# Transformer layer on one core: later constants, the second x tile and query projection ahead of kv, a seven-step Newton, one score matmul per group, and the last down product and norm in column halves

## The chip, the cores and the metric

The kernel runs on one core of a Trainium2 chip. Its time is device microseconds of one execution. The kernel before takes 1866.86 us (median of 3 runs, 1866.0 to 1867.02). The profile is of another single execution, which took 1868.12 us; its span, from the first to the last instruction, is 1866.4 us. The engines are PE (TensorE), DVE (VectorE), ACT (ScalarE), POOL (GpSimd) and SP (SyncE), which here only issues DMAs.

## What is computed

One layer in float32: attention with rotary embedding and causal mask, a residual and a layer norm, then a gated feed-forward part with ternary weights, a residual and a second layer norm. Batch 4, sequence 512, width 1024, 32 query heads on 8 key/value heads, feed-forward width 3584.

```python
q, k, v = x @ wq, x @ wk, x @ wv              # 32 / 8 / 8 heads of 32
q, k = rope(q), rope(k)
attn = softmax(mask(q @ k.T / sqrt(32))) @ v
x = layernorm(x + attn @ wo)                  # (x - mean) / sqrt(var + 1e-5)
gate, up = x @ (gate_t * gate_s).T, x @ (up_t * up_s).T
x = layernorm(x + (silu(gate) * up) @ (down_t * down_s).T)
```

## The kernel before

**Numbers.** The float32 operands of the large products are split into a high and a low float16 part, and a product is made of two or three float16 matmuls. The high part of a loaded page (128 x 1024 float32, 512 KB) is made by ACT (L1109), the low part by DVE (L1231). PE accumulates in eight banks of 512 float32 columns.

**Order.** A planner (`Plan`, L190) holds each piece of work with an engine, a rank, an assumed duration and what it comes after. `close` runs through all pieces as a list scheduler and writes out one fixed order for each engine. On the chip each engine works through its order; semaphores say when a piece may start, and an engine that waits holds everything behind it. So a piece given another duration or place can move others on all engines.

**The start.** ACT first issues six DMAs of constants (L1094 to L1099): two identities, the causal mask, the rope table, and the scales of gate and up. Only then does it load its function table and split pages. SP issues the first twelve pages in the order `FIRST` (L68): x tile 0, two halves of the first quarter of wq, four pages of wkv, then x tiles 1 to 3 and the second quarter of wq. PE's order for unit 0 (L296) is query tile 0, key/value tile 0, query tile 1, key/value tile 1, and so on; a query group is 24 matmuls of 256 columns, a key/value group 24 of 512 (L948). After a group DVE rotates it (L1252 to L1254), POOL adds (L1437), ACT and DVE split it (L1126, L1261), and SP issues a transposing DMA (L1532).

**Attention.** 16 units of 8 heads. `score_q` (L960) gives the row maxima, which go through a small DMA into two extra rows of the query stack; `score_k` (L984) gives the transposed scores for exp on ACT (L1139); POOL masks the diagonal block (L1443) and adds tiles ahead of the row sums (L1451); PE multiplies by v (L998). `score_k` issues one matmul for each head: four times 4 heads of 512 to 128 columns over the four key tiles, grouped by `KEY_HEADS` 1, 1, 2, 4 into one bank. Between these stand projections as filling. One `bound` piece, with a partition reduction on POOL (L1468), scales the feed-forward part.

**Feed-forward.** Two passes of 8 row tiles. Gate and up are products of a Strassen scheme (L1053), as are most down products of the second pass (L1087); the last down round of a pass is plain (L1074): for each row tile and column half 16 matmuls of 512 columns. DVE multiplies the bank by the down scale (L1414), adds it to the accumulator (L1417) and takes statistics (L1222).

**Norms.** 32 of them, 16 after each part. DVE aggregates the statistics and makes a first guess of the inverse root (L1325 to L1329), POOL refines it in three Newton steps of two instructions (L1458, L1460) and makes the bias and the sign with two more (L1462, L1464), ACT applies it to 128 x 1024 (L1157), SP issues the store (L1634).

Of the kernel before, what the change touches and what calls it, by code (L numbers as in the profile page):

```python
# [12 lines left out]
P = 128  # L13
# [51 lines left out]
QS = 3  # L65
NNAT = 2

FIRST = (("x", 0, 0), ("wq", 0, 0), ("wq", 0, 1), ("wkv", 0, 0), ("wkv", 0, 1), ("wkv", 0, 2), ("wkv", 0, 3), ("x", 0, 1), ("x", 0, 2), ("x", 0, 3), ("wq", 1, 0), ("wq", 1, 1))  # L68
# [69 lines left out]
def down_block(q, m):  # L138

    if plain(DOWN_ROUNDS[q][0]):  # L140
        return divmod(m, 2)
    pair, i = divmod(m, NPR)
    odd, half = DOWN_PRODUCTS[i][3]
    return 2 * pair + odd, half

# [114 lines left out]
def attention_plan(plan):  # L260
# [29 lines left out]
    for s in range(-2, NU):  # L290
        u = s + 2
        items = []
        if u < NU:
            items = [("q", u, t) for t in range(NT)]
        if u < NU and u % UNITS == 0:
            items = [i for t in range(NT) for i in (("q", u, t), ("kv", u // UNITS, t))]  # L296
        at = len(items) // 2
        items[at:at] = [("out", t, half) for t, slot in enumerate(OUT_SLOTS) if slot == s for half in range(2)]
        total = sum(PROJ_US[i[0]] for i in items)
        begun = 0.0  # L300
        for item in items:
            groups.append((SLOT * (s + begun / total), SLOT * PROJ_US[item[0]] / total, item))
            begun += PROJ_US[item[0]]
# [155 lines left out]
def ffn_plan(plan):  # L459
# [91 lines left out]
    for d, (q, m) in enumerate(DOWNS):  # L551
# [26 lines left out]
        if h and part == ND - 1:  # L578
            normed(plan, TILES + tile, [("acc", q, m)], at + one + 1)
            put(SY, at + one + 8, .4, "out_store", tile, moves=PAGE_MOVES, after=[("norm", TILES + tile)])  # L580
# [43 lines left out]
def block_kernel(nc, xT, x, wq, wkv, wo, gateT, upT, downT, gate_s, up_s, down_s,  # L624
# [16 lines left out]
    with ctx:  # L641
# [15 lines left out]
        stats = sb(ctx, "stats", [2, 2, 6], F32)  # L657
# [61 lines left out]
        s_const, s_scale, s_set = sem("const_dma"), sem("scale_dma"), sem("const_set")  # L719
# [15 lines left out]
        s_res, s_stat, s_newton, s_norm = sem("residual"), sem("norm_stat"), sem("newton"), sem("normed")  # L735
        s_x1 = [sem(f"x1_store_dma{i}") for i in range(2)]
# [12 lines left out]
        s_last, s_half, s_out = sem("last_added"), sem("half_stats"), sem("out_dma")  # L749
# [26 lines left out]
        assert list(ln_n) == [w[0] for k, w in plan.order[PO] if k == "newton"] == [w[0] for k, w in plan.order[SC] if k == "norm"]  # L776
# [127 lines left out]
        def tensor_program(e):  # L904
# [12 lines left out]
            for kind, which in plan.order[PE]:  # L917
# [34 lines left out]
                elif kind == "score_q":  # L952
# [3 lines left out]
                    on.wait_ge(s_const, 64)  # L956
# [8 lines left out]
                elif kind == "max_tr":  # L965
                    u = which[0]
                    on.wait_ge(s_part, 2 * (u + 1))
                    on.wait_ge(s_const, 64)
# [5 lines left out]
                elif kind == "score_k":  # L974
# [82 lines left out]
                elif kind == "down":  # L1057
# [5 lines left out]
                    if plain(rounds[0]):  # L1063
                        i, h = divmod(m, 2)
                        cols = slice(h * HALF, (h + 1) * HALF)
                        on.wait_ge(s_hlo, HID_BASE[rounds[-1] + 1])
                        for r, c in itertools.product(rounds, range(2)):
# [5 lines left out]
                            for a in range(2):  # L1073
                                t = nc.tensor.matmul(to[:, :], hid_p[place_of(r)][:, k, a, i // 2 * P:(i // 2 + 1) * P],  # L1074
                                                     wd_p[place_of(r)][:, c, cols], start=r == rounds[0] and c == a == 0,
                                                     stop=r == rounds[-1] and c == a == 1)
# [15 lines left out]
        def scalar_program(e):  # L1092
            on = Waits(e)
            e.dma_start(idH[:, :], identH).then_inc(s_const, 16)  # L1094
            e.dma_start(idB[:, :], identB).then_inc(s_const, 16)
            e.dma_start(cmask[:, :], causal).then_inc(s_const, 16)
            e.dma_start(tab[:, :, :, :], rope).then_inc(s_const, 16)
            e.dma_start(sg[:, :], gate_s).then_inc(s_scale, 16)
            e.dma_start(su[:, :], up_s).then_inc(s_scale, 16)  # L1099
            for kind, which in plan.order[SC]:  # L1100
                if kind == "split_hi":
                    n = split_n[which]
                    src, arrived, times = page_of(n)
# [48 lines left out]
                elif kind == "norm":  # L1152
# [3 lines left out]
                    on.wait_ge(s_newton, 8 * (n + 1))  # L1156
# [59 lines left out]
        def vector_program(e):  # L1216
# [7 lines left out]
            for kind, which in plan.order[VE]:  # L1224
# [8 lines left out]
                elif kind == "rotate":  # L1233
# [6 lines left out]
                    on.wait_ge(s_const, 64)  # L1240
# [79 lines left out]
                elif kind == "norm_stats":  # L1320
# [3 lines left out]
                    on.wait_ge(s_half, 2 * n + 2)  # L1324
                    nc.vector.bn_aggr(mv[:, slot, :], stats[:, slot, :, :]).then_inc(s_stat, 1)  # L1325
                    on.wait_ge(s_stat, 3 * n + 1)
                    nc.vector.tensor_scalar(v, mv[:, slot, 1:2], EPS, None, ALU.add).then_inc(s_stat, 1)
                    on.wait_ge(s_stat, 3 * n + 2)
                    nc.vector.tensor_scalar(r.bitcast(I32), v.bitcast(I32), -0.5, float(0x5F3759DF),  # L1329
                                            ALU.mult, ALU.add).then_inc(s_stat, 1)  # L1330
                elif kind == "x1_lo":
# [63 lines left out]
                elif kind == "acc":  # L1395
                    q, m = which
                    n, (p, part), (i, h) = DOWN_N[which], divmod(q, ND), down_block(q, m)
                    cols, old = slice(h * HALF, (h + 1) * HALF), DOWN_BEFORE[which]
                    got, dst = down_bank[n % 2], acc[:, i, cols]
# [11 lines left out]
                    else:  # L1411
                        on.wait_ge(s_ds, p + 1)
                        on.wait_ge(s_last, 2 * (p * PT + i) + h - 1)
# [4 lines left out]
                        on.wait_ge(s_last, 2 * (p * PT + i) + h + 1)  # L1418
                        half_stats(TILES + p * PT + i, h, dst)
# [6 lines left out]
        def gpsimd_program(e):  # L1426
# [4 lines left out]
            for kind, which in plan.order[PO]:  # L1431
# [20 lines left out]
                elif kind == "newton":  # L1452
# [3 lines left out]

                    for m, times in enumerate((1.0, -2.0, 16.0)):
                        nc.gpsimd.tensor_scalar(w, r, r, v, ALU.mult, ALU.mult).then_inc(s_newton, 1)  # L1458
                        on.wait_ge(s_newton, 8 * n + 2 * m + 1)
                        nc.gpsimd.tensor_scalar(r, w, 3.0 * times ** 2, r, ALU.subtract, ALU.mult).then_inc(s_newton, 1)  # L1460
                        on.wait_ge(s_newton, 8 * n + 2 * m + 2)
                    nc.gpsimd.tensor_scalar(w, mv[:, n % 2, 0:1], r, 1.0 / 8192.0, ALU.mult, ALU.mult).then_inc(s_newton, 1)  # L1462
                    on.wait_ge(s_newton, 8 * n + 7)
                    nc.gpsimd.tensor_scalar(r, r, -1.0 / 8192.0, None, ALU.mult).then_inc(s_newton, 1)  # L1464
# [47 lines left out]
        def sync_program(e):  # L1512
            on = Waits(e)
            for kind, which in plan.order[SY]:
# [116 lines left out]
                elif kind == "out_store":  # L1631
                    tile = which[0]
                    on.wait_ge(s_norm, norm_n["norm", TILES + tile])
                    e.dma_start(out[tile], acc[:, tile % PT, :]).then_inc(s_out, 16)  # L1634
            on.wait_ge(s_out, 16 * TILES)

# [66 lines left out]
```

## Time and profile before

| | |
|---|---|
| median of the runs | 1866.86 us |
| the profiled execution | 1868.12 us |
| its span | 1866.4 us |
| PE busy | 97% of the span |
| DVE, ACT, POOL busy | 64%, 38%, 29% |
| mean granted clock of TensorE | 0.993 |
| first matmul starts | 8.71 us |
| last matmul ends | 1856.1 us |

Busy shares are averages over the span. The columns of the single views are given with the rows below. In all of them L and a number is a line of the kernel before, and what stands behind "<-" in brackets is what an engine waited for.

### The profile page before, as it was taken

What the parts mean: (1) busy time and instruction counts of PE and PEld (TensorE: products, weight loads), DVE (VectorE), ACT (ScalarE), POOL (GpSimd) and SP (SyncE); (2) the same over time, 40 slices, a digit from 0 to 9 for tenths busy, and PEclk for the clock granted to TensorE, in tenths of its full rate; (3) what the DMA queues carried; (4) which work ended last, traced back from release to release, by engine and by line L of the source; (5) the groups of instructions that cost most, each with busy time, mean ns of one, the idle gap of its engine ahead of it and who ended that gap; (6) DMA issues with size and microseconds to landing.
All of it is one profiled execution on the core that took longest, in us unless ns stands there. A gap on an engine that the chain in (4) does not pass through costs nothing.

```text
span 1866.4 us, 27364 instructions
## 1 busy us (share of the span) xinstructions
PE 1807.0 (97%) x10528; PEld 882.0 (47%) x10528; DVE 1187.7 (64%) x2047; ACT 710.5 (38%) x1112; POOL 543.6 (29%) x845
## 2 busy tenths in 40 slices
PE   7889999999999998999999999999999999999997
PEld 4545655555555543444444444444444444444443
DVE  7877778668768764445544444745656765667645
ACT  5443444444434444436433343342232322222221
POOL 1354546456546564131000000211321211112103
PEclk9999999999999999999999999999999999999999
DMA  8543234334334398557644353649321211232301
GB/s 246 118 103 78 54 85 125 83 80 116 90 52 114 81 212 221 209 208 263 236 171 150 107 195 126 215 148 211 127 66 53 79 66 51 72 104 85 107 12 79
DMA packets 228162, 233.13 MB, mean 125 GB/s; under 512 B 183872, under 2 KB 184128, under 8 KB 228032
## 3 DMA queue, kind: packets, MB, share of 16 engines
q1 hardware_dynamic: 227168, 230.99, 42.2%
q8 instruction: 83, 1.36, 0.3%
q10 hardware_dynamic: 864, 0.39, 0.1%
q14 instruction: 47, 0.39, 0.1%
HBM read 122.55 MB, written 72.88 MB: 105 GB/s over the span
## 4 chain that ended last, share of the span: by engine, by line
PE 85%; DVE 6%; issue 3%; SPq 2%; POOL 2%; ACT 1%; DMA 1%; ACTq 0%; DVEq 0%; POOLq 0%
PE bank L1053 31%; PE bank L948 20%; PE bank L1074 13%; PE bank L1087 6%; PE bank L998 4%; PE bank L960 3%; PE bank L984 3%; PE bank L1013 2%; SPq L1587 2%; DVE down_forms L1391 1%; PE bank L963 1%; DVE gate_blocks L1385 1%; POOL p_tiles L1451 1%; DVE row_max L1267 0%; DVE up_blocks L1375 0%
## 5 line engine op out<-in xcount | busy, mean ns | idle before, releaser
L1053 PE MATMUL bank<-x_forms,weight_forms 128*128 128x512 f16 x3136 | 700.9, 379 | 12.7 <-DVE gate_blocks L1375 4.4
L1053 PEld LDWEIGHTS bank<-x_forms,weight_forms 128*128 128x128 f16 x3136 | 305.3, 98 | 387.0 <-DVE gate_blocks L1375 7.1
L1139 ACT ACTIVATE p_tiles<-bank 128x512 f32<-128x512 f32 (+1 forms) x352 | 193.0, 556 | 276.6 <-PE bank L984 273.5
L1267 DVE TENSOR_REDUCE row_max<-bank 128x1 f32<-128x384 f32 (+3 forms) x352 | 220.0, 636 | 98.2 <-PE bank L963 96.6
L1074 PE MATMUL bank<-down_forms 128*128 128x512 f16 x1152 | 259.6, 381 | 2.4 <-issue 2.4
L948 PE MATMUL bank<-wq_parts,xT_parts 128*128 128x256 f16 x1536 | 219.4, 275 | 8.9 <-DVE wq_parts L1231 8.7
L1410 DVE TENSOR_TENSOR acc<-bank,acc 128x512 f32<-128x512 f32 x188 | 127.6, 687 | 124.2 <-PE bank L1074 64.7
L1443 POOL TENSOR_SCALAR_AFFINE_SELECT p_tiles<-p_tiles 128x128 f32<-128x128 f32 (+2 forms) x352 | 139.0, 403 | 212.2 <-ACT p_tiles L1139 210.9
L1074 PEld LDWEIGHTS bank<-down_forms 128*128 128x128 f16 x1152 | 113.0, 98 | 139.7 <-issue 4.9
L948 PEld LDWEIGHTS bank<-wq_parts,xT_parts 128*128 128x128 f16 x1536 | 144.1, 98 | 56.8 <-issue 14.2
L948 PE MATMUL bank<-wo_parts,att_parts 128*128 128x512 f16 x672 | 170.1, 382 | 0.6 <-DMA att_parts<-att_spill 0.6
L1475 POOL TENSOR_TENSOR acc<-acc,down_forms 128x1024 f32<-128x1024 f32 x16 | 38.8, 2427 | 377.4 <-DVE acc L1410 377.4
L1087 PE MATMUL bank<-down_forms 128*128 128x512 f16 x560 | 133.6, 379 | 1.7 <-DVE down_forms L1391 1.7
L960 PE MATMUL bank<-k_stack,q_stack 96*128 96x512 f16 (+3 forms) x512 | 127.0, 303 | 5.1 <-DVE row_max L1267 5.1
L984 PE MATMUL bank<-q_stack,k_stack 98*128 98x384 f16 (+3 forms) x512 | 126.4, 301 | 4.6 <-ACT p_tiles L1139 3.1
L1451 POOL TENSOR_TENSOR p_tiles<-p_tiles 128x512 f32<-128x512 f32 (+1 forms) x62 | 115.8, 1868 | 49.4 <-PE bank L998 41.3
L1375 DVE TENSOR_TENSOR up_blocks<-bank,up_blocks 128x512 f32<-128x512 f32 x84 | 57.9, 690 | 112.9 <-PE bank L1053 59.6
L1214 ACT ACTIVATE down_forms<-gate_blocks 128x512 f16<-128x512 f32 x102 | 64.0, 628 | 136.4 <-DVE gate_blocks L1385 130.4
L998 PE MATMUL bank<-p_tiles,v 128*32 128x128 f32 (+3 forms) x1024 | 95.4, 453 | 11.6 <-POOL p_tiles L1443 10.4
L1375 DVE TENSOR_TENSOR gate_blocks<-bank,gate_blocks 128x512 f32<-128x512 f32 x84 | 57.8, 688 | 74.8 <-PE bank L1053 65.0
L948 PE MATMUL bank<-wkv_parts,xT_parts 128*128 128x512 f16 x384 | 98.3, 379 | 1.3 <-DVE wkv_parts L1231 1.3
L1458 POOL TENSOR_SCALAR rstd<-rstd 128x1 f32<-128x1 f32 x96 | 34.8, 363 | 220.2 <-DVE rstd L1329 213.8
(114 smaller groups left out, 1999.9 us busy)
## 6 DMA issues: line engine op xcount, KB each, us to landing
weight_forms_spill<-weight_forms SPq DMA_DIRECT2D x28, 896.0 KB, 5.7
weight_forms<-weight_forms_spill SPq DMA_DIRECT2D x28, 896.0 KB, 4.5
x_forms_spill<-x_parts SPq DMA_DIRECT2D x56, 256.0 KB, 2.4
w_page<-gateT SPq DMA_DIRECT2D x28, 512.0 KB, 5.0
w_page<-upT SPq DMA_DIRECT2D x28, 512.0 KB, 4.0
w_page<-downT SPq DMA_DIRECT2D x28, 512.0 KB, 4.3
att_spill<-att_made SPq DMA_DIRECT2D x64, 128.0 KB, 2.1
down_forms<-x_spill SPq DMA_DIRECT2D x16, 512.0 KB, 3.4
```

Source lines behind the costliest of these rows:

```text
L948: t = nc.tensor.matmul(dst, left[:, a, k, rows], right[:, c, k, cols], start=k == 0 and m == 0, stop=last)
L960: nc.tensor.matmul(to[:, h, :], qT[0:STK, u % QS, h0 + h, i * P:n], kT[0:STK, b % 2, kv_of(u, h0 + h), 0:n], start=h == 0, stop=False, ski ...
L984: t = nc.tensor.matmul(to[:, h, :], kT[0:STKM, b % 2, (u % UNITS) * UG + G, lo:lo + P], qT[0:STKM, u % QS, G * REP + h0 + h, lo:S], start= ...
L998: t = nc.tensor.matmul(bank[PV_BANK[q]][h * HD:(h + 1) * HD, lo:S], value, p32[j][:, h, :], start=j == NT - 1, stop=j == 0, tile_position= ...
L1053: t = nc.tensor.matmul(strassen[bank_set(use)][to][:, :], w_form[:, use % 4, A_FORMS[a_form], k * P:(k + 1) * P], xF[:, :, B_FORMS[b_form] ...
L1074: t = nc.tensor.matmul(to[:, :], hid_p[place_of(r)][:, k, a, i // 2 * P:(i // 2 + 1) * P], wd_p[place_of(r)][:, c, cols], start=r == round ...
L1087: t = nc.tensor.matmul(to[:, :], hid_f[r % NF % 3][:, HID_FORMS.index(a_form), a, pair * P:(pair + 1) * P], wd_f[r % NF % 3][:, DOWN_B[b_f ...
L1139: nc.scalar.activation(p32[j][:, h0:h0 + heads, :], bank[5 + m % 2][:, 0:heads * n].rearrange("p (h c) -> p h c", c=n), ACT.Exp, scale=SCO ...
L1267: nc.vector.tensor_reduce(mx[:, u % 2, i, h0:h0 + ROW_HEADS[i]], bank[3 + m % 2][:, 0:ROW_HEADS[i] * n].rearrange("p (h c) -> p h c", c=n) ...
L1410: nc.vector.tensor_tensor(dst, got[:, :], dst, ALU.add).then_inc(s_acc, 1)
L1443: nc.gpsimd.affine_select(out=block, in_=block, compare_op=ALU.is_ge, fill=0.0, base=0, pattern=[[0, KEY_HEADS[j]], [1, P]], channel_multi ...
L1451: nc.gpsimd.tensor_tensor(to, to, p32[j + 1][:, :, :], ALU.add).then_inc(s_pre, 1)
```

## The change

- ACT issues only the rope table ahead of its first split. The identities and the mask are issued ahead of its split of page 10, the two scales ahead of page 14. The rope table has a semaphore of its own.
- x tile 1 is the fourth page loaded, ahead of the wkv pages, and query tile 1 is projected ahead of key/value tile 0.
- `score_k` issues one matmul for all heads of a use in place of one for each head.
- The first guess of the inverse root has its sign and half the variance folded in, so that the norm needs seven instructions instead of eight. The planner's duration of them goes from 2.0 to 2.6.
- The very last down product (row tile 15, right column half) is made as two of 256 columns. The last norm's seven instructions are on DVE instead of POOL; ACT applies it to the left column half, DVE to the right, and each half has its own store.

```diff
-FIRST = (x00, wq00, wq01, wkv00, wkv01, wkv02, wkv03, x01, x02, x03, wq10, wq11)   # names shortened
+FIRST = (x00, wq00, wq01, x01, wkv00, wkv01, wkv02, wkv03, x02, x03, wq10, wq11)
...
+LAST_DOWN = (PASSES * ND - 1, 2 * PT)
+DOWNS.append(LAST_DOWN)
...
+def down_cols(q, m):
+    h = down_block(q, m)[1]
+    if q < LAST_DOWN[0] or m < 2 * PT - 1:
+        return slice(h * HALF, (h + 1) * HALF)
+    quarter = HALF // 2
+    return slice(D - quarter, D) if m == 2 * PT else slice(D - 2 * quarter, D - quarter)
...
+        if u == 0:
+            items[1:3] = reversed(items[1:3])
...
-    put(PO, end + 1, 2.0, "newton", row, after=[("norm_stats", row)])
-    put(SC, end + 4, 1.1, "norm", row, after=[("newton", row)])
+    if row < 2 * TILES - 1:
+        put(PO, end + 1, 2.6, "newton", row, after=[("norm_stats", row)])
+    put(SC, end + 4, 1.1, "norm", row, after=[("newton" if row < 2 * TILES - 1 else "norm_stats", row)])
...
-                    for h in range(KEY_HEADS[j]):
-                        t = nc.tensor.matmul(to[:, h, :], kT[0:STKM, b % 2, (u % UNITS) * UG + G, lo:lo + P],
-                                             qT[0:STKM, u % QS, G * REP + h0 + h, lo:S], start=True, stop=True)
-                    t.then_inc(s_sk, 1)
+                    heads = slice(G * REP + h0, G * REP + h0 + KEY_HEADS[j])
+                    nc.tensor.matmul(to, kT[0:STKM, b % 2, (u % UNITS) * UG + G, lo:lo + P],
+                                     qT[0:STKM, u % QS, heads, lo:S], start=True, stop=True).then_inc(s_sk, 1)
...
-            e.dma_start(idH[:, :], identH).then_inc(s_const, 16)
-            e.dma_start(idB[:, :], identB).then_inc(s_const, 16)
-            e.dma_start(cmask[:, :], causal).then_inc(s_const, 16)
-            e.dma_start(tab[:, :, :, :], rope).then_inc(s_const, 16)
-            e.dma_start(sg[:, :], gate_s).then_inc(s_scale, 16)
-            e.dma_start(su[:, :], up_s).then_inc(s_scale, 16)
+            e.dma_start(tab[:, :, :, :], rope).then_inc(s_tab, 16)
             for kind, which in plan.order[SC]:
                 if kind == "split_hi":
                     n = split_n[which]
+                    if n == NFIRST - 2:
+                        e.dma_start(idH[:, :], identH).then_inc(s_const, 16)
+                        e.dma_start(idB[:, :], identB).then_inc(s_const, 16)
+                        e.dma_start(cmask[:, :], causal).then_inc(s_const, 16)
+                    elif n == NFIRST + 2:
+                        e.dma_start(sg[:, :], gate_s).then_inc(s_scale, 16)
+                        e.dma_start(su[:, :], up_s).then_inc(s_scale, 16)
...
+                    if which[0] != 2 * TILES - 1:
+                        continue
+                    w = rstd[:, slot, 2:3]
+                    for m in range(3):
+                        nc.vector.tensor_scalar(w, r, r, v, ALU.mult, ALU.mult).then_inc(s_newton, 1)
+                        nc.vector.tensor_scalar(r, w, 1.5, r, ALU.subtract, ALU.mult).then_inc(s_newton, 1)
+                    nc.vector.tensor_scalar(w, mv[:, slot, 0:1], r, -1.0, ALU.mult, ALU.mult).then_inc(s_newton, 1)
+                    right = acc[:, PT - 1, HALF:D]
+                    nc.vector.tensor_scalar(right, right, r, w, ALU.mult, ALU.add).then_inc(s_right, 1)
...
+                    if tile == TILES - 1:
+                        e.dma_start(out[tile, :, 0:HALF], acc[:, PT - 1, 0:HALF]).then_inc(s_out, 16)
+                        on.wait_ge(s_right, 1)
+                        e.dma_start(out[tile, :, HALF:D], acc[:, PT - 1, HALF:D]).then_inc(s_last_out, 16)
```

In the diff the waits between the seven instructions on DVE are left out.

## Rows read from the trace of the kernel before

**Rows 1.** The page, busy time of each engine with share and instruction count.

```profile
PE 1807.0 (97%) x10528; PEld 882.0 (47%) x10528; DVE 1187.7 (64%) x2047; ACT 710.5 (38%) x1112; POOL 543.6 (29%) x845
```

**Rows 2.** Waits of PE: line <- releaser: us in total, times, longest.

```profile
PE bank L998 <- POOL p_tiles L1443: 10.4, 7, 3.6
...
PE bank L948 <- DVE wkv_parts L1231: 1.3, 3, 0.8
```

**Rows 3.** Timeline, first 30 us: start, duration, engine, instruction, [idle before <- releaser].

```profile
3.20 0.51 ACTq L1099 DMA_DIRECT2D up_scale<-up_s  x1
...
5.03 1.06 ACT L1109 ACTIVATE xT_parts<-p_tiles 128x1024 f16<-128x1024 f32 x1
...
8.71 5.19 PE L948 MATMUL bank<-wq_parts,xT_parts 128*128 128x256 f16 x24 [8.71 <-DVE wq_parts L1231]
...
13.74 1.46 PE L948 MATMUL bank<-wkv_parts,xT_parts 128*128 128x512 f16 x6
...
16.50 0.63 ACT L1126 ACTIVATE stack_rows<-rope_cos 128x512 f16<-128x512 f32 x1 [2.64 <-POOL rope_cos L1437]
...
20.77 2.78 PE L948 MATMUL bank<-wq_parts,xT_parts 128*128 128x256 f16 x24
...
28.57 2.78 PE L948 MATMUL bank<-wq_parts,xT_parts 128*128 128x256 f16 x24
```

**Rows 4.** DMA issues at 0.79, 1.25 and 2.2 us: size, us to landing.

```profile
p_tiles<-xT SPq DMA_DIRECT2D x1, 512.0 KB, 3.9
...
p_tiles<-wq SPq DMA_DIRECT2D x1, 512.0 KB, 4.9
...
p_tiles<-wkv SPq DMA_DIRECT2D x1, 512.0 KB, 7.8
```

**Rows 5.** Chain of work that ended last, its end: start, us, what.

```profile
1856.15 0.70 DVE down_forms L1414
...
1858.76 0.16 DVE rstd L1329
...
1859.01 0.35 POOL rstd L1458
...
1862.11 1.24 ACT acc L1157
```

**Rows 6.** Groups by line and shape: out<-in xcount | busy us, mean ns | idle before.

```profile
L1252 DVE TENSOR_TENSOR rope_cos<-bank,rope_tab 128x256 f32<-128x256 f32 x80 | 33.4, 418 | 14.3 <-PE bank L948 11.5 <-ACT v L1116 2.7
...
L1327 DVE TENSOR_SCALAR rstd<-mv 128x1 f32<-128x1 f32 x32 | 4.9, 154 | 1.1
...
L1344 DVE TENSOR_SCALAR scale_bounds<-scale_bounds 128x1 f32<-128x1 f32 x1 | 0.2, 205 | 0.0
...
L1202 ACT ACTIVATE gate_blocks<-gate_blocks,gate_scale 128x512 f32<-128x512 f32 x84 | 60.4, 720 | 95.3 <-DVE gate_blocks L1375 95.1
```

**Rows 7.** Windows around the final store: length, busy, clock, DMA share, GB/s.

```profile
1864.20:1865.50 1.30, 0.00 (x0) 0.00 (x0) 0.00 (x0) 0.00 (x0) 0.00 (x0) 0.50 0.99 400
```

**Rows 8.** Timeline, matmuls of 128 columns and of 512 columns back to back.

```profile
37.68 0.39 PE L960 MATMUL bank<-k_stack,q_stack 96*128 96x128 f16 x4
...
1835.66 20.45 PE L1074 MATMUL bank<-down_forms 128*128 128x512 f16 x94
```

**Rows 9.** Timeline, PE behind POOL's norm work in the last attention units.

```profile
704.60 0.43 PE L998 MATMUL bank<-p_tiles,v 128*32 128x128 f32 x8 [1.17 <-POOL p_tiles L1443]
```

**Rows 10.** Timeline around POOL's partition reduction.

```profile
91.70 0.37 POOL L1468 PARTITION_ALL_REDUCE scale_bounds<-scale_bounds  x1 [7.00 <-issue]
...
93.24 1.51 PE L998 MATMUL bank<-p_tiles,v 128*32 128x384 f32 x8 [3.59 <-POOL p_tiles L1443]
...
100.60 1.26 POOL L1451 TENSOR_TENSOR p_tiles<-p_tiles 128x512 f32<-128x512 f32 x1 [7.17 <-issue]
...
105.82 1.93 PE L998 MATMUL bank<-p_tiles,v 128*32 128x512 f32 x8 [3.25 <-POOL p_tiles L1443]
```

**Rows 11.** Window behind it: length, PE, PEld, DVE, ACT, POOL busy, clock, DMA.

```profile
93.00:100.00 7.00, 6.76 (x37) 3.58 (x37) 3.08 (x8) 1.19 (x2) 0.43 (x2) 0.57 0.01 4
```

More of the change, by code:

```diff
@@ L577, in ffn_plan @@
             put(VE, at + one + 5, 1.25, "add_x1", tile, after=[("scale_row", tile), ("last_x1", tile)])
-        if h and part == ND - 1:
+        if h and part == ND - 1 and (q, m) == done_with(q, i):
             normed(plan, TILES + tile, [("acc", q, m)], at + one + 1)
@@ L775, in block_kernel @@
         ln_n = {w[0]: n for n, (k, w) in enumerate([p for p in plan.order[VE] if p[0] == "norm_stats"])}
-        assert list(ln_n) == [w[0] for k, w in plan.order[PO] if k == "newton"] == [w[0] for k, w in plan.order[SC] if k == "norm"]
+        assert list(ln_n) == [w[0] for k, w in plan.order[PO] if k == "newton"] + [2 * TILES - 1] == [w[0] for k, w in plan.order[SC] if k == "norm"]
         def row_of(tile):
@@ L1073, in tensor_program @@
                             for a in range(2):
-                                t = nc.tensor.matmul(to[:, :], hid_p[place_of(r)][:, k, a, i // 2 * P:(i // 2 + 1) * P],
+                                t = nc.tensor.matmul(to[:, 0:cols.stop - cols.start], hid_p[place_of(r)][:, k, a, i // 2 * P:(i // 2 + 1) * P],
                                                      wd_p[place_of(r)][:, c, cols], start=r == rounds[0] and c == a == 0,
@@ L1155, in scalar_program @@
                     to = row_of(tile)[:, :] if which[0] < TILES else acc[:, tile % PT, :]
-                    on.wait_ge(s_newton, 8 * (n + 1))
+                    on.wait_ge(s_newton, 7 * (n + 1))
+                    if which[0] == 2 * TILES - 1:
+                        to = to[:, 0:HALF]
                     nc.scalar.activation(to, to, ACT.Identity, bias=rstd[:, slot, 2:3], scale=rstd[:, slot, 1:2]).then_inc(s_norm, 1)
@@ L1397, in vector_program @@
                     n, (p, part), (i, h) = DOWN_N[which], divmod(q, ND), down_block(q, m)
-                    cols, old = slice(h * HALF, (h + 1) * HALF), DOWN_BEFORE[which]
-                    got, dst = down_bank[n % 2], acc[:, i, cols]
+                    cols, old = down_cols(q, m), DOWN_BEFORE[which]
+                    got, dst = down_bank[n % 2][:, 0:cols.stop - cols.start], acc[:, i, cols]
                     on.wait_ge(s_down, n + 1)
@@ L1417, in vector_program @@
                         nc.vector.tensor_tensor(dst, dst, last[:, cols], ALU.add).then_inc(s_last, 1)
-                        on.wait_ge(s_last, 2 * (p * PT + i) + h + 1)
-                        half_stats(TILES + p * PT + i, h, dst)
+                        on.wait_ge(s_last, added + 1)
+                        if p * PT + i < TILES - 1:
+                            half_stats(TILES + p * PT + i, h, dst)
+                            continue
+                        for a in range(cols.start, cols.stop, HALF // 2):
+                            half_stats(2 * TILES - 1, a // (HALF // 2), acc[:, i, a:a + HALF // 2])
                 elif kind == "add_x1":
@@ L1455, in gpsimd_program @@
                     on.wait_ge(s_stat, 3 * (n + 1))
-                    for m, times in enumerate((1.0, -2.0, 16.0)):
+                    for m in range(3):
                         nc.gpsimd.tensor_scalar(w, r, r, v, ALU.mult, ALU.mult).then_inc(s_newton, 1)
[L1459 to L1464, printed above, removed]
+                        on.wait_ge(s_newton, 7 * n + 2 * m + 1)
+                        nc.gpsimd.tensor_scalar(r, w, 1.5, r, ALU.subtract, ALU.mult).then_inc(s_newton, 1)
+                        on.wait_ge(s_newton, 7 * n + 2 * m + 2)
+                    nc.gpsimd.tensor_scalar(w, mv[:, n % 2, 0:1], r, -1.0, ALU.mult, ALU.mult).then_inc(s_newton, 1)
                 elif kind == "bound":
```

41 lines of the change are left out of this document (25 added, 16 removed).

## The prediction

> **What bounds the kernel.** I read the busy times first, then PE's waits, then the timeline of both ends. PE is busy for 97% of the span [rows 1], so this is a kernel in which only three things count: PE's work, the gaps inside it, and the two ends where PE has nothing. The gaps inside are few: the largest group is 10.4 us behind POOL's masking, 1.3 us behind the wkv splits [rows 2]. The ends are larger. At the start PE idles until 8.71 us [rows 3]; at the end 10.3 us of the span lie behind its last matmul, a serial chain from DVE to POOL to ACT to the store [rows 5]. Elsewhere the other engines run beside PE, and what they gain is worth nothing unless PE waits for it.
>
> **The start: constants.** ACT issues six DMAs, the last at 3.20 for 0.51 us, then loads its table, and its first split starts at 5.03 [rows 3]. The x page landed at 0.79 + 3.9 = 4.7 [rows 4], so late issue costs ACT about 0.3 us. But PE's first matmul needs the wq page too: issued at 1.25, landed 4.9 later, at 6.15 [rows 4]; then 1.06 of ACT and some 1.2 of DVE with hops of 0.1. That gives PE a start at 8.6 however early x is ready. With 124 KB of constants out of the way the page may land up to 0.3 earlier, but the rope table, 256 KB, is now ahead and pushes back. I take 0.1, between 0 and 0.4.
>
> The moved issues cost ACT some 0.5 us each. Three of them now stand ahead of the split of page 10, near 22 us, where ACT is busy. What is queued behind is a split for unit 1 and the rotated rows of unit 0; the first scores that need those start at 37.7 [rows 8], so 1.4 us is covered. If rotations fell behind by that much PE would wait for a bank, up to 0.7. The scales are issued near 32 us, where ACT waits for pages, and are first read far later.
>
> **The start: order.** The first 24 matmuls of 256 columns take 5.19 us, the same 24 at 20.77 take 2.78 [rows 3]: a pace of 0.214 against 0.109 us. The column of the granted clock reads 1.00 in both, but 256 columns in 0.214 us is the 1.2 GHz level and in 0.109 the 2.4 GHz level; at 13.74 the full level is there. So the first query group costs 5.03 us in both kernels. Then before: the key/value group runs from 13.74 to 20.77, 7.03 us, of which 24 x 0.216 = 5.2 are work and the rest is waits for the wkv splits (1.3, [rows 2]) and refills. Query tile 1 follows, then key/value tile 1, and query tile 2 starts at 28.57.
>
> After: x tile 1 is the fourth page, where a wkv page landed at 2.2 + 7.8 = 10.0 [rows 4]; split by 12.5, it is ready when query tile 0 ends at 8.6 + 5.03 = 13.6. Its group runs at full pace to 16.2. The wkv pages come 1.3 us later each than now, and the key/value group starts 2.5 later. It isn't free of waits: ACT works in order and stands 2.64 us behind POOL's slow addition [rows 3], now probably ahead of wkv page 2 rather than 3, and so that page's halves would be ready at 19.2 against 18.8 when PE asks. I allow 0.4. The sum: 8.6 + 5.03 + 2.6 + 5.2 + 0.4 + 5.2 = 27.0 for the start of query tile 2, against 28.57. **Start: -1.5 us**, between -0.7 (ACT blocks twice) and -2.1 (no wait at all).
>
> **The end.** PE's work there is the same: 16 x 0.216 against 32 x 0.109, 0.03 more. The two parts share the banks in turn, and DVE has let go of the first 3.5 us earlier. Behind PE:
> - Multiply, add, statistics: three pieces of 0.70 now [rows 5], with hops 2.18 us. With 256 columns from a bank DVE takes 0.418 [rows 6]. The statistics at 256 don't occur; between 0.35 (half) and 0.70, I take 0.42. 3 x 0.42 + 0.07 = 1.33: **-0.85**. The first quarter's chain is over in the 1.7 us of the second's matmuls.
> - Aggregation and guess stay.
> - Newton: from the end of DVE's guess at 1858.92 to ACT's start at 1862.11, 3.19 us for POOL's eight instructions [rows 5]. On DVE a 128x1 instruction takes 0.154 with constants, 0.205 with one operand from memory [rows 6]; two such operands don't occur, by the same step 0.257, at most POOL's 0.34. With hops of 0.035: 3 x (0.257 + 0.205) + 0.205 + 7 x 0.035 = 1.84: **-1.3**, between -1.0 and -1.6.
> - Applying it: 1.24 for 1024 columns [rows 5]; a 512-column ACT instruction with a scale from memory takes 0.72 [rows 6]. I take 0.75: **-0.5**. DVE's right half is beside it.
> - The store: the second is issued some 0.4 us after the first. The data of the one store move for 1.3 us at 400 GB/s, ending 0.5 ahead of the landing [rows 7]. The first half would move for 0.65 and the second can start as it ends, so nearly nothing is lost: **+0.1**, between 0 and +0.4.
>
> Together **-2.5 us**, between -1.7 and -3.0.
>
> The Trainium skill, page "DMA: Bandwidth & Descriptors", section "Anatomy of one DMA", gives a DMA 2.0 us plus its bytes at 436 GB/s; that is for GpSimd's path, and this trace's store lands 2.6 us after issue where the rule makes 3.2. By the rule a 256 KB store takes 2.6 us, 0.4 later issued 3.0, a gain of 0.2 where I have a loss of 0.1; the measurement decides.
>
> **Scores.** Four matmuls of 128 columns take 0.39 us of which 0.224 is the last one's own, a pace of 0.0555; 94 of 512 take 20.45, a pace of 0.216 [rows 8]. So four small ones cost 0.222 against 0.216, and two of 256 0.218. Over 32 groups with one use of the first kind and two of the second: 32 x (0.006 + 2 x 0.002) = **-0.3 us**, between 0 and -0.6; what each needs in waits is unchanged.
>
> **Newton elsewhere.** 31 norms lose one POOL instruction of 0.22 plus a hop. PE feels it where POOL's masking stands behind a norm: I find one such place, 1.17 us of PE's wait at 704.60 [rows 9], behind eight such instructions. **-0.25**, between 0 and -0.5.
>
> **Sum.** -1.5 - 2.5 - 0.3 - 0.25 = -4.55. The profiled execution's 1868.12 would be 1863.6; it lies 1.26 above the median of the runs, so the median goes from 1866.86 to **1862.3 us**. Measurement tells about 0.2% (3.7 us, 1863.1) from no change, so the forecast lies just beyond that bound.
>
> **The rivals** all concern the planner, which writes new orders because of the swapped groups and of 2.6 for 2.0.
> - *The start's gain is not kept.* PE's filling is taken from the same queue of projections, and if the page loads or unit 0's chain through row maxima and its DMA, not PE, set the first scores, 1.5 us only become idle time by 70 us. For it: that chain runs through DVE and a DMA, which the change doesn't speed. Against: with PE busy for 97% [rows 1], none of its larger waits [rows 2, 10] lies ahead of 89 us, so PE would start each group as early as it is free. 1866.86 - 3.05 = 1863.8. With it I count other small shuffles of +1 to +4: 1864 to 1866.
> - *Slower.* POOL stands still for 7.00 us ahead of the partition reduction and 7.17 behind it, without an instruction [rows 10]. PE covers part of each with work already fed: it waits only 3.59 the first time, and 3.25 at 105.8 [rows 10]. Then the clock falls: the window behind shows 0.57 [rows 11], which is the 1.2 GHz level for 6 of 7 us. If the new order puts the reduction where nothing is fed, the cover of 3.4 + 3.9 us is gone, and another 3.4 us of work at half pace costs 1.7: +9.0. 1862.3 + 9.0 = 1871.3. It decides from a loss of cover of about 8 us, that is in both gaps.
> - *Clearly faster.* The same mechanism the other way: if one of the two gaps gets full cover, 3.4 us of wait go and 1.7 us at the low level with it, -5: 1857.3.
>
> The page "GPSIMD Engine Reference" of the Trainium skill tells of about 6 us for the first call of a freshly loaded kernel with no visible instruction; these gaps of 7.0 and 7.2 agree, and by it they are neither shortened nor removed by this change.
>
> **Chances.** Forecast 0.48 (own range 1861.2 to 1864; of it 0.35 beyond 0.2%), gain not kept or small shuffles 0.25, slower 0.12, clearly faster 0.15. So faster 0.50, same 0.38, slower 0.12. The range goes from 1857.5 to 1867.0: below it lies the tail of the last case, above it the slower one.
>
> **What would show it.** Query tile 2's matmuls start at 27.0, with under 0.5 us of waits for wkv. From PE's last matmul to ACT's last end 4.6 us instead of 7.2, store included 7.7. PE's waits at 90 to 106 us near 6.8 us in sum, with two stretches at the low clock. If the start gains and PE's idle time at 60 to 110 grows by as much, the first rival holds. I am wrong if those POOL gaps move, or if new low-clock stretches appear that aren't there now.

## The result and the profile after

The changed kernel takes 0.9976 of the time of the one before, with a 95% interval of 0.9967 to 0.9985 (20 runs of each, medians 1865.1 and 1868.97 us; the three runs known at the prediction lay at the lower side of the kernel before). Forecast was 1862.3 of 1866.86, the same 0.9976. The runs of the kernel before lie up to 15 us apart, and they do so with TensorE's clock: over the 35 of them measured beside the first four experiments the shortest, 1861.7 us, has a mean granted clock of 0.996, the longest, 1876.1, one of 0.988, and time and clock are correlated by -0.88. So a single profile carries some microseconds of chance, and what follows separates stages of the profile, which repeat, from times, which need intervals.

The profiled execution of after has a span of 1862.9 us against 1866.4. The waits of PE (line <- releaser: us in total, times, longest), answering to [rows 2]:

```profile
PE bank L964 <- DVE wq_parts L1249: 8.9, 1, 8.9
PE bank L1013 <- POOL p_tiles L1482: 8.3, 4, 2.7
...
PE bank L964 <- DMA att_parts<-att_spill: 2.1, 1, 2.1
...
PE bank L964 <- DVE wkv_parts L1249: 0.9, 2, 0.7
```

Of the single groups two changed most: 2.1 us less behind POOL's masking, 1.5 us more behind a load of attention parts (0.6 in the kernel before). All waits of PE from query tile 2 on sum to 35.1 us against 38.0; how much of that is chance is told behind the experiments. Part of it is an exchange. Where PE stood 1.17 us behind POOL's norm work [rows 9], no such wait is left, and one for a DMA has grown beside it:

```profile
703.25 4.00 PE L964 MATMUL bank<-wo_parts,att_parts 128*128 128x512 f16 x9 [2.09 <-DMA att_parts<-att_spill]
```

The start, timeline of after (start, duration, engine, instruction, [idle before]), answering to [rows 3]:

```profile
0.79 0.41 ACTq L1108 DMA_DIRECT2D rope_tab<-rope  x1
...
4.97 1.06 ACT L1125 ACTIVATE xT_parts<-p_tiles 128x1024 f16<-128x1024 f32 x1 [2.46 <-DMA p_tiles<-xT]
...
8.87 7.04 PE L964 MATMUL bank<-wq_parts,xT_parts 128*128 128x256 f16 x48 [8.87 <-DVE wq_parts L1249]
...
15.74 2.75 PE L964 MATMUL bank<-wkv_parts,xT_parts 128*128 128x512 f16 x12
15.89 0.63 ACT L1142 ACTIVATE stack_rows<-rope_cos 128x512 f16<-128x512 f32 x1 [3.27 <-POOL rope_cos L1476]
...
19.19 1.47 PE L964 MATMUL bank<-wkv_parts,xT_parts 128*128 128x512 f16 x6 [0.70 <-DVE wkv_parts L1249]
...
20.86 6.65 PE L964 MATMUL bank<-wkv_parts,xT_parts 128*128 128x512 f16 x30 [0.20 <-DVE wkv_parts L1249]
...
27.35 2.78 PE L964 MATMUL bank<-wq_parts,xT_parts 128*128 128x256 f16 x24
```

ACT is done with its DMA issue and its table early and then waits 2.46 us for the x page. PE starts at 8.87, no earlier than the 8.71 before, and query tile 2 at 27.35 against 28.57.

The end, the chain of work that ended last (start, us, what), answering to [rows 5]:

```profile
1854.80 0.44 DVE down_forms L1449
...
1855.26 0.44 DVE acc L1452
...
1855.72 0.44 DVE stats L1240
...
1856.18 0.28 DVE mv L1344
...
1856.67 0.17 DVE rstd L1349
...
1856.93 0.28 DVE rstd L1357
...
1857.24 0.22 DVE rstd L1359
...
1858.60 0.22 DVE rstd L1361
...
1858.85 0.81 ACT acc L1175
```

From PE's last matmul (1854.78) to ACT's last end 4.88 us where there were 7.23, and to the end of the span 8.12 where there were 10.28.

POOL around the partition reduction, timeline of after, answering to [rows 10]:

```profile
89.77 0.48 POOL L1504 PARTITION_ALL_REDUCE scale_bounds<-scale_bounds  x1 [6.71 <-issue]
...
98.31 3.74 POOL L1490 TENSOR_TENSOR p_tiles<-p_tiles 128x512 f32<-128x512 f32 x2 [6.70 <-issue]
```

The two standstills are there as before, 1.9 and 2.3 us earlier in the span, and PE's waits behind them are 2.73 and 2.69 us in this execution.

### The profile page after: what moved, and what is told of

It reads as the page before. It is cut to its first block, busy times and chain, and to the rows that moved or that the text cites. A ratio compares the mean times of both kernels' runs of the same rounds, so it can differ in the third digit from the quotient of the medians.

```text
span 1862.9 us, 27050 instructions
## 1 busy us (share of the span) xinstructions
PE 1808.5 (97%) x10384; PEld 875.0 (47%) x10384; DVE 1187.1 (64%) x2059; ACT 709.8 (38%) x1112; POOL 529.4 (28%) x806
## 4 chain that ended last, share of the span: by engine, by line
PE 87%; DVE 6%; issue 2%; SPq 2%; DMA 1%; POOL 1%; ACT 1%; DVEq 0%; ACTq 0%; POOLq 0%
PE bank L1068 32%; PE bank L964 20%; PE bank L1088 13%; PE bank L1101 6%; PE bank L1013 4%; PE bank L976 3%; PE bank L1000 3%; PE bank L1028 2%; PE bank L979 1%; DVE down_forms L1425 1%; SPq L1623 1%; DVE gate_blocks L1419 1%; DVE row_max L1285 0%; DVE up_blocks L1409 0%; DVE down_forms L1402 0%
## 5 line engine op out<-in xcount | busy, mean ns | idle before, releaser
L1088 PE MATMUL bank<-down_forms 128*128 128x512 f16 (+1 forms) x1168 | 259.6, 378 | 2.4 <-issue 2.4
L1101 PE MATMUL bank<-down_forms 128*128 128x512 f16 x560 | 133.6, 379 | 1.7 <-DVE down_forms L1425 1.7
L1000 PE MATMUL bank<-q_stack,k_stack 98*128 98x512 f16 (+1 forms) x352 | 126.5, 365 | 3.8 <-ACT p_tiles L1155 2.6
```

What stands on the lines that cost most here:

```text
L1000: nc.tensor.matmul(to, kT[0:STKM, b % 2, (u % UNITS) * UG + G, lo:lo + P], qT[0:STKM, u % QS, heads, lo:S], start=True, stop=True).then_in ...
L1088: t = nc.tensor.matmul(to[:, 0:cols.stop - cols.start], hid_p[place_of(r)][:, k, a, i // 2 * P:(i // 2 + 1) * P], wd_p[place_of(r)][:, c, ...
L1101: t = nc.tensor.matmul(to[:, :], hid_f[r % NF % 3][:, HID_FORMS.index(a_form), a, pair * P:(pair + 1) * P], wd_f[r % NF % 3][:, DOWN_B[b_f ...
```

## The experiments

All ratios are to the kernel before, measured beside it on the same chip. The experiments ran in three groups, each on another chip: e1 to e4, e5 to e8 and e9 to e12 as numbered below, beside a kernel before with medians of 1868.9, 1867.7 and 1871.8 us. Times in us are therefore compared only inside a group.

**The parts alone.** Is the gain kept, and whose is it? First the start alone: the new `FIRST`, the swapped groups and the later constants, on the kernel before.

> Only the start of the change: constants later, x tile 1 as fourth page, query tile 1 ahead of key/value tile 0; no other part. My theory (the start's gain is kept to the end): query tile 2's matmuls start near 27.35 us as in the changed kernel, 1.2 us earlier than the 28.57 before, and the time falls by 1.2 to 1.5 us (ratio 0.9993). Rival (gain lost behind unit 0's chain of row maxima or in POOL's standstill): the 1.2 us at 28 us are there, but PE's last matmul ends where it did, 1856 us in the span, ratio 1.000.

Measured (e1): 0.9994 (0.9978 to 1.0009). This can't tell the theory's 0.9993 from the rival's 1.000. In its profile query tile 2 starts at 27.21 us, PE's last matmul ends at 1852.8, 3.3 us earlier than before; 3.4 us of that are the clock's (6.8 us lost to the 1.2 GHz level against 10.2, reckoned as for the table of stages below), so the profile doesn't decide it either.

The end and the seven-step norm, with `put(PO, end + 1, 2.0, "newton", ...)` as before, so that the orders of all engines stay (one down product more, one norm less on POOL):

> The end of the change and the seven-step norm with the planner's old price of 2.0; the orders of all engines are those of before but for one more down product. Theory: 2.2 to 2.5 us less behind PE's last matmul (10.3 before, 8.1 after) and nothing or up to 0.5 us ahead of it, ratio 0.9986. Rival (the seven-step norm helps PE where POOL's masking stands behind a norm): the last matmul ends more than 1 us earlier too, ratio 0.998 or less.

Measured (e2): 0.9993 (0.9979 to 1.0006). Behind PE's last matmul 8.06 us, the 2.2 us that were expected; the interval of the time holds the theory's 0.9986 as well as no change. The rival isn't seen: without the planner's new price PE's waits behind POOL's masking, those at the standstills left out, are 3.3 us here and 3.6 in the kernel before. This profile also shows how much POOL's standstill can cost in one execution, PE's second wait behind it:

```profile
108.64 1.93 PE L1012 MATMUL bank<-p_tiles,v 128*32 128x512 f32 x8 [6.23 <-POOL p_tiles L1479]
```

The merged score matmuls alone:

```diff
-for h in range(KEY_HEADS[j]):
-    t = nc.tensor.matmul(to[:, h, :], kT[...], qT[0:STKM, u % QS, G * REP + h0 + h, lo:S], start=True, stop=True)
+nc.tensor.matmul(to, kT[...], qT[0:STKM, u % QS, heads, lo:S], start=True, stop=True)
```

> Only the score matmuls of all heads of a use in one, all orders as before. Theory: PE saves the pace of small matmuls alone, 0.3 us (ratio 0.9998), not measurable in the time; in the profile the groups of that line have the same sum. Rival (each weight load saved is worth its own time, 160 x 0.1 us beside busy PE): 5 us or more, ratio 0.997.

Measured (e3): 1.0009 (0.9996 to 1.0021). Against what was expected it leans to slower, but the interval holds no change. The rival (5 us or more gained) is excluded. In the profile PE's weight loads of this line fall from 512 to 352 and from 45.8 to 33.8 us, while the line's matmuls are busy for 126.3 us against 127.5: the loads lay beside the matmuls.

> The changed kernel itself, beside the parts on the same chip. If the parts simply add up, its gain is that of the start (1.2), of the end (2.2) and of the scores (0.3), 3.7 us, ratio 0.9980; what is missing or over is what the planner's new price of the norm and the joint new order give.

Measured (e4): 0.9979 (0.9968 to 0.9989). The parts give 0.9994, 0.9993 and 1.0009, together 0.9996, the whole 0.9976 and 0.9979. Since each part is uncertain by 0.0014, their sum is by some 0.0025, so this is no contradiction, but it is no proof of adding up either. The parts leave out the planner's new price of the norm, which comes next.

**The norm's seven steps and its price in the planner, alone** (`7 * n` in the waits, folded constants, 2.6 for 2.0):

> The kernel before with only the seven-step norm on POOL and the planner's price of 2.6. Theory (few waits of PE stand behind norms): 0 to 0.5 us less, ratio 0.9998. Rival (the planner's new order in the attention part, 54 of PE's 2420 pieces moved, is what makes the changed kernel's times lie closer together, 1864 to 1869 against 1862 to 1876): the spread of this kernel's runs is as small, and the ratio is 0.9985 or less.

Measured (e7): 0.9997 (0.9984 to 1.0011). The runs spread from 1862 to 1872, as before: the rival falls. The one instruction less shows only at the end, 9.98 us behind PE's last matmul instead of 10.3.

**The scores again, by taking them out of the changed kernel:**

> The changed kernel with one score matmul for each head as before; the rest of the change stays. The part alone read 1.0009. If merging costs time, this is faster than the changed kernel by 1 to 2 us, ratio to before 0.997; if it was noise, it is slower by 0.3, ratio 0.998.

Measured (e8): 0.9986 (0.9972 to 0.9999), on the other side of the changed kernel's 0.9979 than the part alone would have it. So there is no sign that merging costs anything; the likeliest reading of e3's lean is chance.

**What POOL's standstill costs.** The slower and the clearly faster rival both rest on it. First it was taken away, with all orders kept; this kernel leaves out the maximum over partitions:

```diff
-nc.gpsimd.partition_all_reduce(sc[:, 2:4], sc[:, 0:2], P, bass.bass_isa.ReduceOp.max)
+nc.gpsimd.tensor_copy(sc[:, 2:4], sc[:, 0:2])
```

> The changed kernel with the partition reduction on POOL replaced by a plain copy of each partition's own value, all orders kept. This leaves out the maximum over partitions, so the scale of the feed-forward part is another one. Theory: POOL's two standstills of 7 us are the loading of code for that reduction and back, and go with it: PE's two waits of 2.7 to 3.6 us each at 88 to 108 us and the low clock behind them disappear, 8 to 11 us less than the changed kernel, ratio to before 0.992 to 0.994. Rival (the standstill belongs to something else at that place, or the run-to-run clock takes it back): less than 3 us, ratio 0.9965 or more.

Measured (e5): 0.9925 (0.9908 to 0.9941), 1855.1 us. POOL goes straight on, and PE has no wait left there (timeline of POOL):

```profile
81.58 2.53 POOL L1482 TENSOR_SCALAR_AFFINE_SELECT p_tiles<-p_tiles 128x512 f32<-128x512 f32 x3
84.06 1.17 POOL L1504 COPY scale_bounds<-scale_bounds 128x2 f32<-128x2 f32 x1
85.94 0.61 POOL L1482 TENSOR_SCALAR_AFFINE_SELECT p_tiles<-p_tiles 128x128 f32<-128x128 f32 x2 [0.71 <-ACT p_tiles L1155]
```

Against the changed kernel's 0.9979 that is 0.0054, 10 us for one instruction of 0.37 us; the changed kernel with separate score matmuls (e8), on the same chip, has a median 10.1 us longer. The profiles show where it goes. In the changed kernel PE waits 5.4 us behind the two standstills, and then its clock is down. A window of the changed kernel and the same window of this one, columns as in [rows 11]:

```profile
88.00:112.00 24.00, 18.58 (x127) 9.82 (x120) 11.93 (x30) 6.15 (x11) 8.68 (x16) 0.79 0.12 26
```

```profile
88.00:112.00 24.00, 23.80 (x218) 14.27 (x215) 22.30 (x45) 13.23 (x23) 15.51 (x21) 1.00 0.42 86
```

A granted clock of 0.79 over 24 us is 5 us of PE's work lost, 1.00 is none; that makes 10.4 us with the waits. The loss there is 5.1 us in seven of the eight profiles with the reduction (3.6 in e2's, where the stretch runs on past 112 us) and nothing in the six without it. The standstills belong to the reduction.

Then the same with the computation kept. Two small DMAs and DVE make the maximum over partitions:

```diff
+elif kind == "bound_store":
+    on.wait_ge(s_bound, 1)
+    e.dma_start(bound_dram[:, :], sc[:, 0:2]).then_inc(s_bdma, 16)
+elif kind == "bound_load":
+    on.wait_ge(s_bdma, 16)
+    e.dma_start(all_bounds[:, :], bound_dram.rearrange("p c -> (p c)").partition_broadcast(P)).then_inc(s_bdma, 16)
...
+on.wait_ge(s_bdma, 32)
+nc.vector.tensor_reduce(sc[:, 2:4], all_bounds[:, :].rearrange("p (n c) -> p c n", c=2), mybir.AxisListType.X, ALU.max)
```

> The changed kernel with the maximum over partitions made without POOL: each partition's pair goes to memory in one DMA, all 128 pairs come back to every partition in a second, and DVE reduces them. It computes the reference. Theory: as in the run without the reduction, since DVE, SP and the DMA queues have room there; ratio to before 0.992 to 0.994. Rival: SP's order holds the second DMA and what is queued behind it for the 2 to 3 us of the first, and DVE waits on both, which PE feels: half of the gain is lost, ratio 0.996.

Measured (e6): 0.9913 (0.9895 to 0.9930), 1853.8 us. The rival's 0.996 is excluded. SP issues the store and the load three microseconds apart, and DVE reads the result late and without waiting (timelines of SP and DVE; DMA issues with KB and us to landing):

```profile
78.69 0.34 SPq L1563 DMA_DIRECT2D bound_spill<-scale_bounds  x1
81.92 0.32 SPq L1566 DMA_DIRECT2D all_bounds<-bound_spill  x1
...
96.20 0.40 DVE L1383 TENSOR_REDUCE scale_bounds<-all_bounds 128x2 f32<-128x256 f32 x1
```

```profile
all_bounds<-bound_spill SPq DMA_DIRECT2D x1, 128.0 KB, 4.2
bound_spill<-scale_bounds SPq DMA_DIRECT2D x1, 1.0 KB, 3.2
```

**The change on the base without the reduction.** The same edit on the kernel before:

> The kernel before with the maximum over partitions made by two small DMAs and DVE in place of POOL, nothing of the change. With POOL's standstills gone the runs should lie close together, so that what the change itself is worth shows as the distance to the changed kernel with the same edit (ratio to before 0.9913). Theory: 0.24% above that, 0.9937. Rival (the change's gain comes from how its order meets the standstills): the two are alike, 0.991 to 0.992.

Measured (e9): 0.9929 (0.9913 to 0.9944). The runs don't lie close together, as was hoped: 1852.8 to 1862.1 us. The changed kernel with it had 0.9913, so the change is worth 0.0016 here, with intervals that would hold anything from none to 0.004. These two ran on different chips, and by the medians of all runs e6 would have 0.9925, so this distance is weak. On one chip this kernel has a median of 1858.3 us, and the next two, which are the changed kernel but for one part each, have 1855.5 and 1855.9: 2.8 and 2.4 us less, near the 2.2 of the end. The rival (gain only through the standstills) isn't excluded by the ratios; the stages below exclude it for the end.

> The changed kernel with the DMA bound, but with the start as before: all constants first, x tile 1 after wkv, key/value tile 0 ahead of query tile 1. From the profiles so far query tile 2 starts at 28.4 with the old start and at 27.9 with the new one. Theory: the start is worth 0.5 us, not 1.5; ratio 0.9916. Rival (as predicted): 1.5 us, ratio 0.9921.

Measured (e10): 0.9914 (0.9900 to 0.9928). Taking the start out costs nothing that can be measured; query tile 2 starts at 27.85 in its profile.

> The changed kernel with the DMA bound, but one score matmul for each head; same orders. Theory: 0.3 us slower than with merged ones, ratio 0.9915, hardly to be told from 0.9913. Rival (merging costs, as the part alone read): 1 us or more faster, ratio 0.9908 or less.

Measured (e11): 0.9916 (0.9903 to 0.9930), 0.0003 above the kernel with merged ones, as expected and inside the noise.

**Who delays the first matmul.** In `scalar_program` the rope table is issued ahead of the second split:

```diff
-e.dma_start(tab[:, :, :, :], rope).then_inc(s_tab, 16)
 for kind, which in plan.order[SC]:
     if kind == "split_hi":
         n = split_n[which]
+        if n == 1:
+            e.dma_start(tab[:, :, :, :], rope).then_inc(s_tab, 16)
```

> The changed kernel with the DMA bound, and the rope table issued ahead of ACT's second split instead of first of all. Theory: the 256 KB of the table no longer stand in the way of the first wq page, PE's first matmul starts at 8.6 or 8.7 instead of 8.9 to 9.4, query tile 2 at 27.4, and the table still lands ahead of the first rotation at 13.3; ratio 0.9910. Rival (pages, not the table, set the first matmul): it starts at 9.0 as before, or the rotation waits for the table and the gain is lost.

Measured (e12): 0.9906 (0.9892 to 0.9920), 1853.6 us, the lowest ratio of all kernels here, though not to be told from the 0.9913 to 0.9916 of the other changed kernels with the DMA bound. Its timeline:

```profile
4.35 1.06 ACT L1131 ACTIVATE xT_parts<-p_tiles 128x1024 f16<-128x1024 f32 x1 [2.27 <-DMA p_tiles<-xT]
4.36 0.38 ACTq L1117 DMA_DIRECT2D rope_tab<-rope  x1
...
8.18 4.21 PE L969 MATMUL bank<-wq_parts,xT_parts 128*128 128x256 f16 x19 [8.18 <-DVE wq_parts L1255]
```

The x page is there at 4.35 instead of 4.97 to 5.49 in the seven other profiles of the new start, the first matmul at 8.18, and query tile 2 at 27.01. The table has landed at 10.5, ahead of the first rotation at 12.99, which waits for PE and not for it. It is one profile, but both starts lie below those of all thirteen others; the theory holds, and by more than it said.

**The stages over all profiles**, in us. First matmul and query tile 2 are starts in the timeline, the tail is the span less the end of PE's last matmul:

| kernels | first matmul | query tile 2 | tail |
|---|---|---|---|
| old start (before, e2, e3, e7, e9, e10) | 8.71 to 8.87, mean 8.79 | 27.85 to 28.68, mean 28.32 | |
| new start (after, e1, e4, e5, e6, e8, e11) | 8.87 to 9.40, mean 9.14 | 27.21 to 28.70, mean 27.96 | |
| new start, rope late (e12) | 8.18 | 27.01 | |
| old end (before, e1, e3, e9) | | | 10.27 to 10.32 |
| new end (after, e2, e4, e5, e6, e8, e10, e11, e12) | | | 8.03 to 8.12 |

Between them, from query tile 2's first matmul to the end of PE's last, stand PE's waits and the work; a part of the work runs at the 1.2 GHz level. What that costs is estimated as the sum of (1 - granted clock) x length over windows of 2 us:

| kernel | stage | PE's waits in it | lost to the low level | rest |
|---|---|---|---|---|
| before | 1827.5 | 38.0 | 10.2 | 1779.3 |
| after | 1827.4 | 35.1 | 15.4 | 1776.9 |
| after, again (e4) | 1827.4 | 39.5 | 10.2 | 1777.7 |
| all fourteen | 1812.9 to 1832.8 | 29.0 to 42.8 | 5.1 to 15.4 | 1776.9 to 1779.6 |

The rest is the same within 3 us in all fourteen profiles, though the stages differ by 20 us: nearly all of the difference between two profiles is waits and clock. Two profiles of the same changed kernel differ by 4.4 us in the waits and by 5.2 in the clock.

## Why the prediction came out right, and where it didn't

**The end: right, -2.2 for -2.5.** This term carries the result, and it repeats within 0.1 us over nine profiles. Its pieces, by the steps of the prediction: multiply, add and statistics 1.38 us (1.33 said); the aggregation over four groups 0.28 for 0.22, which was said to stay; from the guess to ACT's start 2.02 (1.84 said), where the two-operand instruction takes 0.273 us (0.257 said), and a hop of 0.10 stands at the beginning, which was not in the sum; ACT's half 0.81 (0.75 said); the store 3.24 behind ACT's end for 3.05, so 0.2 lost (0.1 said). Each is a little over, none is wrong in kind.

**The start: mechanism only half right, -0.4 for -1.5.** The pair of profiles on the table, 27.35 against 28.57, looks like a hit, and is chance: over thirteen profiles the means differ by 0.36 us. On the side of before 28.57 was 0.25 above the mean. On the side of after the sum said 27.0, the mean is 27.96: the first matmul 9.14 instead of 8.6, the two query groups 7.27 instead of 7.63, the rest up to query tile 2 11.55 instead of 10.8. Two steps failed. The first is "I take 0.1, between 0 and 0.4" for PE's start: the first matmul is on the average 0.35 later, not 0.1 earlier. I had credited the 124 KB that leave and only mentioned the 256 KB that now come first (in the kernel before the table landed at 9.6 us, in the changed one at 5.1); the run with the rope table later shows them to be the larger, 0.7 to 1.2 us. ACT's six issues, the visible stall of the kernel before, had been hiding behind the page's landing. The second is "I allow 0.4" for the waits in the key/value group. From its first matmul to query tile 2 pass 11.6 us in six of seven profiles, 10.4 of them work; the rest is 0.90 us of waits for wkv and 0.3 of refills. The order of events was the one foreseen (ACT stands 3.27 us behind POOL's addition ahead of wkv page 2), its price was twice to three times as high. The stated sign, under 0.5 us of waits for wkv, is not met.

The two query groups softened this. The change to the 2.4 GHz level comes at another matmul in each execution: the first query group of the old order takes 4.26 to 5.03 us in six profiles, where 5.03 was taken for a constant, and the two groups of the new order 6.5 to 8.1. Either order hands this on. In the old one 14.83 us pass from the first key/value matmul to query tile 2 in all six profiles, with the same waits for wkv, however early the group starts; in the new one they take 11.6 us in all but one (e8), where 0.3 us of the delay is made up.

**Scores: -0.3, not told apart from nothing.** Alone 1.0009, taken out 0.9986 against 0.9979, on the base without the reduction 0.9916 against 0.9913. The three lie on both sides of nothing and each is uncertain by 2 us or more, so they hold the forecast and can't confirm it. What is excluded is that 160 weight loads fewer are worth their own time: 12 us of loads went, and 5 us or more would have shown.

**Newton elsewhere: -0.25, not seen.** The one place found did lose its wait, and beside it stands a DMA of the attention parts, 2.09 us where 0.6 had been. The step read the wait behind POOL and didn't ask what is late next. Over the profiles the exchange repeats and gains nothing: PE's waits behind masking, those at the standstills left out, are 3.3 to 3.8 us in the four with the price of 2.0 and the reduction (before, e1, e2, e3) and 2.9 in the four with 2.6 (after, e4, e7, e8); those for attention parts 0.6 to 2.0 and 1.7 to 3.3. It follows the planner's price, not the instruction that went: e2 has seven steps and 3.3. At the end the instruction is worth its 0.3.

**The rivals.** PE's waits at the standstills are 5.4 us in sum against 6.8, and 6.6 in the second profile of the changed kernel; the two stretches at the low clock are there in both. So neither the slower nor the faster case came. A sign of being wrong did appear, a new stretch at the low clock at 236 us in the profile of after; but other executions of either order have such stretches too, at 68, 244, 824 or 1362 us, so it says nothing. That it is PE's most expensive neighbour was right: taking it away gives 10 to 13 us. The first rival said that the start's gain would not be kept; in truth there was hardly one to keep.

**The sum.** The stages account for -0.4 and -2.2, that is -2.6 us or 0.9986. The times say 0.9976 and 0.9979, with upper ends of 0.9985 and 0.9989. So 1.3 to 1.9 us of the measured gain have no stage that shows them. They must lie between query tile 2 and PE's last matmul, where the pair of profiles shows 0.1 us only because 2.9 us fewer waits and 5.2 us more at the low clock nearly cancel with 2.4 us of rest. PE's waits there are 35.8 to 42.8 us in the four profiles with the old price and the reduction, mean 39.1, and 35.1 to 39.5 in the four with the new one, mean 36.7; on the base without the reduction 32.2 (e9) and 32.1 (e10) with the old start, 29.0 to 30.5 (e5, e6, e11, e12) with the new. That leans to the planner's new order being worth a microsecond or two, but the ranges of the first comparison overlap, the second has two profiles on one side, and e10's time (0.9914) is no worse than that of the others. The total agreed with the forecast partly because this part, forecast at -0.55, stands in for the start: in the number that is luck. Whether it is the planner's new order, or chance, stays open. So does why the changed kernel's runs lie closer together (standard deviation 1.7 us against 3.0 in the twenty runs of each, 1.2 against 3.4 in e4's group): with the start alone it is 3.3, with the price of the norm alone 3.2.

## What to carry to other kernels

At the end of a kernel everything is serial, and there the small prices count: a chain of tiny instructions costs less on DVE than on POOL (2.0 us for the seven of a Newton refinement, 2.9 for the same seven on POOL in e7, 3.2 for the eight of before), and halving the last tile's columns takes time off each engine it passes. At the start look for the transfer that the first matmul needs, and put nothing in front of it; an engine's own stall there may hide behind that transfer. An instruction that costs 0.4 us in the list can cost ten around it: look for idle time that ends with no releaser before and behind a custom operation. And before two profiles are compared by their ends, take PE's waits and the time lost to the low clock out of both: here one kernel's two profiles differ by 4 to 5 us in each.

## What the runs showed of the hardware

- POOL stands still for 6.2 to 7.3 us ahead of the partition reduction and for 6.7 to 7.6 us behind it, in all eight profiles that have it. Behind it five masking instructions still run at once (92.15 us in the kernel before); the second standstill comes ahead of the next addition. The page "GPSIMD Engine Reference" of the Trainium skill (section "Instruction dispatch") gives about 6 us for the first call of newly loaded code. The standstill ahead agrees in size; that code is loaded in it is not seen in the traces, and they show as long a standstill again behind the reduction, of which that section says nothing.
- One reduction of 0.37 us was worth 10 us (copy in its place, all orders kept: 5.4 of waits, 5 of lost clock) to 13 us (DMA in its place, on the kernel before, with new orders).
- At the start the granted clock reads 1.00 throughout, while matmuls of 256 columns follow each other at 0.214 us, the 1.2 GHz level, and then at 0.109 us.
- The mean granted clock differs by 0.008 between the runs of one kernel; 0.008 of 1868 us is 15 us, and the runs are 14.5 us apart. In the profile of the kernel before, stretches at the 1.2 GHz level stand at 92 to 100, 104 to 110, 706 to 710, 730 to 734 and 1798 to 1804 us. The first two stand behind PE's waits at the reduction and are in all eight profiles that have it but for the first one in e2's; the others come and go from execution to execution.
- Two operands from memory make a 128x1 instruction of DVE 0.27 us, one 0.21, none 0.15.
